# Per-subject matrix plus residual, 128 batches on one core: loads released by stores alone, looped PE and Pool programs, additions on tiles of two

## The reference

```python
def reference(x, itok_B_0_7, L0_cond_weights):   # (128,128,1024), (128,) int32, (8,128,128)
    w = L0_cond_weights[itok_B_0_7]
    return x + jnp.einsum('bct,bcd->bdt', x, w)
```

## Time and profile before

| what | us |
|---|---|
| median of three runs | 330.94 |
| span of the profiled execution, first to last instruction | 329.6 |
| PE busy with matmuls | 240.7 |
| DVE busy | 156.7 |
| Pool busy | 37.7 |

### The profile page before, as it was taken

One profiled execution on the slowest core, in us unless ns is written; L12 is line 12 of the kernel. 1 busy time (PEld: TensorE's weight loads), 2 busy tenths in 40 slices (PEclk: granted clock), 3 DMA queues, 4 the chain that ended last, 5 costly groups with the idle time before them and its releaser, 6 DMA issues.

```text
span 329.6 us, 2144 instructions
## 1 busy us (share of the span) xinstructions
PE 240.7 (73%) x512; PEld 94.4 (29%) x512; DVE 156.7 (48%) x128; POOL 37.7 (11%) x132
## 2 busy tenths in 40 slices
PE   2987768667786986776776777876866866866880
PEld 1432323223332332232232232232332322322330
DVE  0564454454354544545545445445445445445451
POOL 1332234443333100000000000000000000000000
PEclk9999999999799899999999999999999999999997
DMA  7999999999999999999999999999999999999996
GB/s 266 331 381 420 421 421 421 421 421 419 421 421 420 420 420 421 419 421 421 421 420 421 421 421 420 421 418 421 420 421 421 421 421 419 422 421 421 421 417 253
DMA packets 35933, 134.87 MB, mean 409 GB/s; under 512 B 2129, under 2 KB 3154, under 8 KB 35922
## 3 DMA queue, kind: packets, MB, share of 16 engines
q1 hardware_dynamic: 18480, 67.64, 50.7%
q10 hardware_dynamic: 17442, 67.11, 49.7%
HBM read 67.63 MB, written 67.11 MB: 409 GB/s over the span
## 4 chain that ended last, share of the span: by engine, by line
DMA 69%; PE 22%; DVE 6%; issue 1%; POOLq 0%; POOL 0%
DMA x_ring<-x 68%; PE product L99 22%; DVE x_ring L111 6%; DMA weight_bank<-weights 1%; POOLq L83 0%; POOLq L84 0%; POOL weight_of_batch L84 0%; POOLq L80 0%
## 5 line engine op out<-in xcount | busy, mean ns | idle before, releaser
L99 PE MATMUL product<-x_ring,weight_of_batch 128*128 128x512 f32 x512 | 240.7, 616 | 81.3 <-DMA x_ring<-x 74.7
L111 DVE TENSOR_TENSOR x_ring<-product,x_ring 128x1024 f32<-128x1024 f32 x128 | 156.7, 1225 | 166.6 <-PE product L99 166.6
L99 PEld LDWEIGHTS product<-x_ring,weight_of_batch 128*128 128x128 f32 x512 | 94.4, 193 | 226.8 <-DMA x_ring<-x 129.8
L84 POOL COPY weight_of_batch<-weight_bank 128x128 f32 x128 | 37.5, 293 | 72.1 <-issue 72.1
L130 POOL MEMSET const-float32-0.0<- 128x1 f32 x1 | 0.1, 98 | 0.2 <-issue 0.2
L130 POOL MEMSET const-bfloat16-1.0<- 128x1 bf16 x1 | 0.1, 101 | 0.0
L130 POOL MEMSET const-uint8-127<- 128x1 uint8 x1 | 0.1, 101 | 0.0
L130 POOL MEMSET const-float32-1.0<- 128x1 f32 x1 | 0.1, 98 | 0.0
## 6 DMA issues: line engine op xcount, KB each, us to landing
x_ring<-x SPq DMA_DIRECT2D x62, 1024.0 KB, 14.9
out<-x_ring ACTq DMA_DIRECT2D x62, 1024.0 KB, 13.0
x_ring<-x SPq DMA_DIRECT2D x4, 512.0 KB, 8.1
out<-x_ring ACTq DMA_DIRECT2D x4, 512.0 KB, 5.8
weight_bank<-weights SPq DMA_DIRECT2D x1, 512.0 KB, 4.4
subject_row<-subjects ACTq DMA_DIRECT2D x1, 0.5 KB
```

Source lines behind the costliest of these rows:

```text
L84: pool.tensor_copy(weight_of_batch[:, b, :], weight_bank[:, bass.ds(subject, 1), :]).then_inc(picked, 1)
L99: last = pe.matmul(product[b % PRODUCTS][:, cols], weight_of_batch[:, b, :], x_ring[:, slot, k, cols], start=True, stop=True)
L111: dve.tensor_tensor(x_ring[:, slot, k, :], product[b % PRODUCTS][:, :], x_ring[:, slot, k, :], mybir.AluOpType.add).then_inc(added, 1)
```

## The change

- All tiles hold two batches, 64 tiles in 8 laps over the ring; the single-batch tiles at both ends are gone.
- SP waits before a load only for the store that frees its place. The wait for the sums of tile t-4 is gone.
- PE and Pool run a hardware loop over the 8 laps, with the 8 places written out inside; their semaphore waits compare against register values made from the lap number. PE waits once per tile for each of the three semaphores.
- Pool copies into `weight_ring`, which has 16 places, and so waits per tile until PE has done with the tile eight earlier (`multiplied`). It raises `picked` once per tile. The index is read at an address made from the lap number.
- A PSUM product now holds a tile of two (four banks), and there are two of them. DVE makes one addition of 128x2048 per tile, and PE's tile t waits for the addition of tile t-2.
- `multiplied` and `added` start at 8 and at 2, raised by PE and DVE at their start.

```diff
-    TILES = tile_batches(B, PER_TILE, ramp=[1, 1])
+    TILES = B // PER_TILE
+    LAPS = TILES // SLOTS
-    PRODUCTS = PSUM_BANKS // BANKS
+    PRODUCTS = PSUM_BANKS // (BANKS * PER_TILE)
...
-        weight_of_batch = ctx.enter_context(nc.sbuf_tensor("weight_of_batch", [C, B, D], f32))
+        weight_ring = ctx.enter_context(nc.sbuf_tensor("weight_ring", [C, LAP_BATCHES, D], f32))
-        product = [ctx.enter_context(nc.psum_tensor(f"product{i}", [D, T], f32)) for i in range(PRODUCTS)]
+        product = [ctx.enter_context(nc.psum_tensor(f"product{i}", [D, PER_TILE, T], f32)) for i in range(PRODUCTS)]
...
-            for t, (first, count) in enumerate(TILES):
+            for t in range(TILES):
                 slot, lap = t % SLOTS, t // SLOTS
-                if t >= AHEAD:
-                    sp.wait_ge(added, sum(TILES[t - AHEAD]))
                 if lap:
                     sp.wait_ge(x_out[slot], DMA_INC * lap)
-                sp.dma_start(x_ring[:, slot, 0:count, :],
-                             x[first:first + count, :, :].rearrange("b c t -> c b t")).then_inc(x_in[slot], DMA_INC)
+                sp.dma_start(x_ring[:, slot, :, :], x_of_tile[t]).then_inc(x_in[slot], DMA_INC)
...
-            for b in range(B):
+            with pool.Fori(0, LAPS) as lap:
+                for slot in range(SLOTS):
-                subject = pool.value_load(subject_row[0:1, b:b + 1], min_val=0, max_val=S - 1)
-                pool.tensor_copy(weight_of_batch[:, b, :],
-                                 weight_bank[:, bass.ds(subject, 1), :]).then_inc(picked, 1)
+                    pool.wait_ge(multiplied, lap * SLOTS + (slot + 1))
+                    for k in range(PER_TILE):
+                        n = slot * PER_TILE + k
+                        subject = pool.value_load(subject_row[0:1, bass.ds(lap * LAP_BATCHES + n, 1)],
+                                                  min_val=0, max_val=S - 1)
+                        copied = pool.tensor_copy(weight_ring[:, n, :], weight_bank[:, bass.ds(subject, 1), :])
+                    copied.then_inc(picked, 1)
...
+            pe.sem_inc(multiplied, SLOTS)
+            with pe.Fori(0, LAPS) as lap:
+                for slot in range(SLOTS):
+                    pe.wait_ge(picked, lap * SLOTS + (slot + 1))
+                    pe.wait_ge(added, lap * SLOTS + (slot + 1))
+                    pe.wait_ge(x_in[slot], lap * DMA_INC + DMA_INC)
+                    for k in range(PER_TILE):
+                        for n in range(BANKS):
+                            cols = slice(n * PSUM_BANK_COLS, (n + 1) * PSUM_BANK_COLS)
+                            last = pe.matmul(product[slot % PRODUCTS][:, k, cols],
+                                             weight_ring[:, slot * PER_TILE + k, :],
+                                             x_ring[:, slot, k, cols], start=True, stop=True)
                     last.then_inc(multiplied, 1)
...
+            dve.sem_inc(added, PRODUCTS)
+            for t in range(TILES):
                 slot = t % SLOTS
+                dve.wait_ge(multiplied, SLOTS + t + 1)
+                dve.tensor_tensor(x_ring[:, slot, :, :], product[t % PRODUCTS][:, :, :], x_ring[:, slot, :, :],
+                                  mybir.AluOpType.add).then_inc(added, 1)
...
-                act.wait_ge(added, first + count)
+                act.wait_ge(added, PRODUCTS + t + 1)
+                act.dma_start(out_of_tile[t], x_ring[:, slot, :, :]).then_inc(x_out[slot], DMA_INC)
```

More of the change, by code:

```diff
@@ L20 @@
 DMA_INC = 16
[L23 to L30, removed]
+PER_TILE = 2
+SLOTS = 8
 def subject_residual_kernel(nc, x, subjects, weights, out):
```

13 lines of the change are left out of this document (5 added, 8 removed).

## The result

| | before | changed |
|---|---|---|
| median of the runs shown, us | 331.03 (330.94 to 331.30, 4 runs) | 327.76 (327.08 to 327.94, 4 runs) |
| ratio, 95% interval | | 0.9897 (0.9883 to 0.9911) |
| span of the profiled execution, us | 329.6 | 326.3 (that execution took 327.94) |

The changed kernel is faster by 3.3 us, 1.0%. The forecast was 328.5 with a range of 327.3 to 330.6.

The account below looks back on a forecast made before the run. The prediction took the kernel to be bound by its transfers at 421 GB/s. From 329.6 us, -2.5 (hole) and +0.15 (end) gave 327.2 us of span, 328.5 us as a median (+1.3), range 327.3 to 330.6.

Parts of the forecast that it names:

- the unused 9.2 us: Whole span before the change: transfer time not used, 329.6 us of span against 320.4 us for all bytes at 421 GB/s.
- the term for 10:20: Window 10 to 20 us, hole at 12:14: loads waiting for stores only cover it, -2.5 us.
- Two of the signs named beforehand: Start: 10:20 at about 415 GB/s or more, and SP issuing eight loads by 6 us, would show the forecast right.
- 66 tiles become 64: 0: Tile count: four transfers fewer, lying side by side, so 0.
- PE's loop ... on the path 0: PE's three register waits per tile: 0.46 us, under 1.29 us of cover, so 0 on the path; jumps back also covered.
- The end: +0.15: Stores alone at the end: 2.4 MB more pass at 410 GB/s instead of 421, +0.15 us.
- The last stores run dry: End: stores' backlog falls below 10.6 us, 2.1 us are idle, 330.6 us; chance 14%.
- the margin of 1 us: End: 11.6 us of stores still to pass against 10.6 us until tile 63's store flows, so engines stay busy.
- PE becomes the bound: PE's three waits before each tile: at 0.52 us each a tile takes 5.26 us, median 357 us; chance 6%.
- The hole only moves: Start: eight loads not taken at once or store 0 late, an equal hole opens later, 330.9 us; chance 4%.
- the rate rises: Steady stretch: deeper queues raise the rate from 421 to 434 GB/s, median 318.8 us; chance 3%.

Follow-up runs that it names:

- the 240 waits: The changed kernel with 240 more waits on register values per tile on PE, after the wait for the load: 868.48 us, ratio 2.6235.

## Why the prediction was right

**The bound and the hole: right.** The transfers bound both kernels at 421 GB/s, and the change worked on the unused 9.2 us. -2.5 us was the term for 10:20; the windows of the changed kernel give -2.3, and -2.1 when it was measured again (403 GB/s). The wait of the four tiles 5 to 8 alone makes the hole, shown by keeping it for them and for the others. Two of the signs named beforehand were missed, without harm: 10:20 stayed below 415 GB/s, and the eighth load was issued at 6.7 us instead of by 6, since one issue took 2.2 us.

**Isolated, that term was over-sized.** Removing the wait from the kernel before gave 1.9 us. The step "the hole at 10:20 is covered: -2.5 us" took the whole loss of the window for the wait's; 0.6 us of it ((421 - 395) / 421 x 10) stay. This is not the small tiles' doing alone: with uniform tiles and no wait it is 0.5 us (399 GB/s), and in the profiles of the changed kernel 0.3 and 0.4.

**"66 tiles become 64: 0" was wrong:** 0.56 us. The transfers lie side by side in the steady stretch, as the step says, but not where the single-batch tiles are, at the ends; 0.3 us of it is seen from 318 us on, 0.1 at 10:20.

**"PE's loop ... on the path 0": right for the waits, incomplete for the loops.** Register waits are free here: eight more changed nothing, and the trace shows them made during the matmuls of the tile before. Each of many added waits took 53 ns of the sequencer, where 152 had been assumed. A jump back was recorded as 76 to 225 ns, median 208, where the prediction had named 108. But the step only asked what a loop adds, and not what it takes away: the looped kernel is 0.4 to 1.3 us faster than the written-out one, as large as the uniform tiles' part or larger. Fewer fetches of program may be a part of it; that is not shown, and the late end of a looped kernel says that they are not all.

**The end: +0.15 was of the wrong sign.** The stretch of stores alone is longer, as predicted, but stores alone are not bound to 410 GB/s. With a store queue of four to five tiles they ran at 421:

```profile
310.00:318.00 8.00, 3.67 (x8) 1.44 (x8) 4.09 (x2) 0.00 (x0) 0.97 1.03 421
```

The 410 of before was measured on a shallower queue; that the depth makes the difference is inferred. The end as a whole gave back 0.8 us (3.3 to 2.5), and 1.5 us when the changed kernel was measured again (1.8). Step by step it loses 3.1 us without the wait, 2.8 with uniform tiles, and 2.8 with merged additions and written-out programs, so deeper queues and uniform tiles gave 0.5 us; the rest is seen in looped kernels alone, and differs from one execution to another.

The errors nearly cancel: 0.6 us too much for the hole, and 0.6 us for the tiles and 0.4 to 1.3 for the programs not counted. So the total of 328.5 against 327.8 was luck in part.

**The rivals.** *The last stores run dry* did not happen in the changed kernel, whose store queue turned out at 23.8 us, deeper than the margin of 1 us suggested; it did happen with the wait put back. *PE becomes the bound* needed 0.43 us per wait and a wait costs 0.05. Its sum was also wrong in kind: it added the waits to the matmuls of every tile, while the sequencer makes them during the matmuls of the tile before, as the 240 waits show. Many waits do slow the kernel, as both kernels show, once the sequencer's own time or the way from an addition to the next matmul is the longest. *The hole only moves* and *the rate rises* found nothing for them: 421 before and after.

## What to carry to other kernels

When transfers bound a kernel, cost each part of a change in the stretches where the DMA engines are not full, and there alone; a wait that is the longest of its engine can be worth nothing in 58 tiles and everything in the first four. A wait that limits how far loads run ahead and small tiles at the ends are tuned together: take one away and the other must be looked at again, and the ring must be deep enough for both queues (eight places lost nothing here, four lost 18%). Written-out programs were slower than looped ones here, by 0.4 to 1.3 us; their fetches go over the same DMA engines, which is a reason to measure both forms in a kernel bound by transfers.

## What was not expected of the hardware

The first store takes long to start. In the changed kernel it was issued at 16.8 us, and its queue (q10) shows no packet of it until 20; between 20 and 21 it has its first:

```profile
q1 hardware_dynamic: 72, 0.28, 70.5%
q10 hardware_dynamic: 30, 0.12, 30.3%
```

That is over 3 us from issue to flow, against 1.9 in the kernel before. The load queue is only part of the difference, since the kernel before begins with a store of half the size. Such a store took 1.9 us when the load queue had run dry and 3.5 us without the wait for sums, with eight loads queued (issued at 11.5, first packets at 15.0 to 15.5). A store of 1 MB took 3.3 us or more with eight loads queued, when the changed kernel was measured again (15.2 to 18.5), and still 2.9 us or more with the wait put back, where nothing was queued when it was issued (16.6 to 19.5). In the changed kernel's first profile it cost nothing, because the loads kept the engines full; measured again, 18:20 ran at 377 GB/s around the first store, and the kernel without the wait ran at 315 at 14:16. Loads alone ran at 410 GB/s, loads and stores together and stores alone with a deep queue at 421.
